# A cross-attention kernel: the last output-weight split one batch later, a norm quarter moved, another division of the beginning, another order of the tail

## The reference

```python
a = layer_norm(ctx) * gamma + beta          # B, T, D = 8, 512, 1024
Q = (x @ Wq.T), K = (a @ Wk.T), V = (a @ Wv.T)      # 16 heads of 64
scores = einsum('bhtd,bhsd->bhts', Q, K) * 64 ** -0.5
scores = where(mask, scores, -inf)
attn = softmax(scores)
out = einsum('bhts,bhsd->bhtd', attn, V)
return x + tanh(gate) * (out.reshape(B, T, D) @ Wo.T)
```

## Time and profile before

| | us |
|---|---|
| median of 3 runs (1995.44 to 1995.61) | 1995.55 |
| the profiled execution's own time | 2000.36 |
| its span (what the trace shows) | 1998.2 |
| PE busy | 1958.0 (98%) |
| DVE busy | 1613.8 (81%) |
| POOL busy | 1462.7 (73%) |
| ACT busy | 1344.3 (67%) |
| TensorE clock granted, mean | 0.994 |

### The profile page before, as it was taken

One profiled execution on the slowest core, in us unless ns is written; L12 is line 12 of the kernel. 1 busy time (PEld: TensorE's weight loads), 2 busy tenths in 40 slices (PEclk: granted clock), 3 DMA queues, 4 the chain that ended last, 5 costly groups with the idle time before them and its releaser, 6 DMA issues.

```text
span 1998.2 us, 26443 instructions
## 1 busy us (share of the span) xinstructions
PE 1958.0 (98%) x8720; PEld 1589.9 (80%) x8720; DVE 1613.8 (81%) x2082; ACT 1344.3 (67%) x2434; POOL 1462.7 (73%) x806
## 2 busy tenths in 40 slices
PE   6899999999999999999999999999999999999997
PEld 5787778888788887888888888888888888888886
DVE  7688768887788877888788887888878888778877
ACT  5768876578756686657865678665876568756554
POOL 4899996668865778666876669767697667966664
PEclk8999999999999999999999999999999999999999
DMA  7577544554355443554445543455433644435422
GB/s 264 174 252 242 189 172 167 220 180 140 130 194 188 168 170 112 212 197 142 151 149 194 191 168 119 163 197 182 175 129 130 253 151 150 154 124 191 164 93 106
DMA packets 136502, 341.96 MB, mean 171 GB/s; under 512 B 55856, under 2 KB 56880, under 8 KB 135472
## 3 DMA queue, kind: packets, MB, share of 16 engines
q1 hardware_dynamic: 136368, 340.28, 48.9%
HBM read 288.86 MB, written 51.36 MB: 170 GB/s over the span
## 4 chain that ended last, share of the span: by engine, by line
PE 79%; POOL 8%; ACT 6%; DVE 4%; issue 1%; DMA 1%; SPq 0%; ACTq 0%; DVEq 0%; POOLq 0%
PE pj L445 14%; PE pj L449 14%; PE pj L447 14%; PE sc L398 5%; PE sc L402 5%; PE sc L399 5%; PE sc L372 5%; PE sc L373 5%; PE pv L392 5%; PE pv L393 5%; POOL a_lo L1138 4%; DVE mq L821 2%; POOL p_lo L1104 2%; PE pj L381 1%; ACT prob L619 1%
## 5 line engine op out<-in xcount | busy, mean ns | idle before, releaser
L1104 POOL TENSOR_TENSOR p_lo<-prob,p_hi 128x1024 fp32r<-128x1024 f32 x255 | 611.4, 2408 | 188.1 <-ACT p_hi L624 188.1
L445 PE MATMUL pj<-a_hi,w_hi 128*128 128x512 f32 x1024 | 404.2, 395 | 7.7 <-DVE v_st L865 3.0
L449 PE MATMUL pj<-a_hi,w_lo 128*128 128x512 f32 x1024 | 401.3, 392 | 0.0
L447 PE MATMUL pj<-a_lo,w_hi 128*128 128x512 f32 x1024 | 401.0, 392 | 0.0
L821 DVE TRANSPOSE_TENSOR_REDUCE mq<-sc 128x32 f32<-128x1024 f32 x256 | 304.0, 1225 | 79.9 <-PE sc L373 79.1
L888 DVE SCALAR_TENSOR_TENSOR xy<-sc,tg_b,xy 128x1024 f32<-128x1024 f32 x244 | 306.2, 1273 | 31.6 <-PE sc L402 25.6
L619 ACT ACTIVATE prob<-prob 128x1024 f32<-128x1024 f32 x256 | 271.4, 1060 | 89.2 <-DVE prob L843 88.8
L843 DVE TENSOR_TENSOR prob<-sc,m_b 128x1024 f32<-128x1024 f32 x256 | 301.6, 1220 | 4.4
L1108 POOL TENSOR_TENSOR prob<-prob 128x1024 f32<-128x1024 f32 x126 | 302.1, 2398 | 0.0
L1115 POOL TENSOR_TENSOR r_b<-o,r_b 128x512 f32<-128x512 f32 x62 | 81.2, 1310 | 267.9 <-DVE r_b L860 267.9
L624 ACT CAST p_hi<-prob 128x1024 fp32r<-128x1024 f32 x256 | 269.5, 1053 | 3.5
(11 more groups left out here) (129 smaller groups left out, 3731.6 us busy)
## 6 DMA issues: line engine op xcount, KB each, us to landing
w_hi<-kept_hi SPq DMA_DIRECT2D x225, 512.0 KB, 3.7
w_lo<-kept_lo SPq DMA_DIRECT2D x225, 512.0 KB, 4.6
xy<-in_xT SPq DMA_DIRECT2D x32, 512.0 KB, 6.6
cx<-in_ctx SPq DMA_DIRECT2D x32, 512.0 KB, 7.4
kept_hi<-w_hi SPq DMA_DIRECT2D x32, 512.0 KB, 5.3
kept_lo<-w_lo SPq DMA_DIRECT2D x32, 512.0 KB, 6.0
out_y<-xy SPq DMA_DIRECT2D x7, 2048.0 KB, 9.8
w_raw<-in_wq SPq DMA_DIRECT2D x8, 512.0 KB, 5.1
```

Of the source, the lines that this page charges most:

```text
L445: pe.matmul(dst, w_hi[:, w, cols], s_hi[:, i], start=i == 0, stop=False)
L447: pe.matmul(dst, w_hi[:, w, cols], s_lo[:, i], start=False, stop=False)
L449: mm = pe.matmul(dst, w_lo[:, w, cols], s_hi[:, i], start=False, stop=i == KT - 1)
L1104: pool.tensor_tensor(p_lo[:, 2 * i:2 * i + 2], prob[:, h, 2 * i:2 * i + 2], f32(p_hi[:, 2 * i:2 * i + 2]), ALU.subtract).then_inc(pl_done, 1)
```

## The change

Five edits.

- The split of WO 7 leaves body 6. Its raw load goes out at the start of body 8, POOL makes its low part at the end of body 8, ACT its high part in body 9 ahead of the maxima, as for the other WO splits, into WO's own slot. SP's waits and stores around it move with it, and body 9 no longer loads WO 7 back.
- In batch 0 alone, the norm quarters of (5,0) and (6,0) stand behind `hand_out_maxima` on ACT instead of ahead of `gather_maxima`.
- In the beginning, DVE computes variance plus epsilon (two tiny instructions) and normalises with the mean itself, so that ACT has no `moments` there.
- In the beginning, the low parts of WK 0 and WV 0 are made by DVE (`first_split`), not by POOL; the two mask rows stand behind all of `a_low` and `q_low` instead of ahead of them, and `q_low` behind `a_low`; ACT casts slices 2, 4 and 6 instead of 2 and 5.
- In the tail, the last value matmuls and key sums stand ahead of the output pair that waits for DVE, and POOL makes the whole last low part of the probabilities (128 x 1024) where DVE had made half of it (L1035).

```diff
-FIRST_HIGH = (2, 5)
+FIRST_HIGH = (2, 4, 6)
...
-BODY_SPLITS += [[(WV, PAIRS - 1), (WO, PAIRS - 1), (WO, PAIRS - 3)], [(WO, PAIRS - 2)]]
+BODY_SPLITS += [[(WV, PAIRS - 1), (WO, PAIRS - 3)], [(WO, PAIRS - 2)], [(WO, PAIRS - 1)]]
...
         def out_split(k):
-
-            b, j = divmod(k - 1, PAIRS)
-            return b, WO, j - 1
+            return (0, WO, k - 2) if 2 <= k < PAIRS + 2 else (1, WO, 0)
...
             def batch(b):
                 for j in range(PAIRS):
                     k = b * PAIRS + j
+                    if k == PAIRS:
+                        m = NUMBER[WO, PAIRS - 1]
+                        sp.dma_start(w_raw[:, m % 2], wts[WO][PAIRS - 1]).then_inc(w_ld[m % 2], 16)
+                        keep_split(m - 1)
+                    if k == PAIRS + 1:
+                        keep_split(NUMBER[WO, PAIRS - 1])
                     load_kept(WV, (j + 1) % PAIRS, k)
                     exchange_sums(k - 1)
                     load_kept(WQ, (j + 2) % PAIRS, k)
                     load_kept(WK, (j + 2) % PAIRS, k)
-                    load_kept(WO, (j - 1) % PAIRS, k)
+                    if k == PAIRS + 1:
+                        sp.wait_ge(w_out[WO], 32 * PAIRS)
+                    if k > PAIRS:
+                        load_kept(WO, (j - 1) % PAIRS, k)
...
                 values(k, 1, 0)
                 pe.wait_ge(oadd_done, k * 2 + 1)
                 key_sums(1, 0, pv[0][:, 0])
+                values(k, 1, 1)
+                key_sums(1, 1, pv[0][:, 0])
                 pe.wait_ge(acc_done, 4 * k - 6)
                 out_pair(k - 2, 3, lower, done=False)
-                pe.wait_ge(plv_done, 1)
-                values(k, 1, 1)
-                key_sums(1, 1, pv[0][:, 0])
...
-                if (j, 0) in NORM and b < B - 1:
+                if (j, 0) in NORM and 0 < b < B - 1:
                     norm_quarter(b, NORM[j, 0])
                 if kind == "switch":
                     for i in range(KT // 2):
                         a_high(k, b, i)
                 gather_maxima(k, 0)
                 hand_out_maxima(k, 0)
+                if (j, 0) in NORM and b == 0:
+                    norm_quarter(b, NORM[j, 0])
...
                 split_w(b, WQ, j + 2)
                 if kind == "prepare":
-                    split_w(b, WO, PAIRS - 1, WQ)
                     for i in range(KT // 2, KT):
                         x_high(k, b, i, (b + 1) % 2)
...
-            moments(-1, 0)
-            moments(-1, 1)
             q_high(-1, 0)
             q_high(-1, 1)
...
-                dve.wait_ge(ph_done, k * 4 + 4)
-                dve.tensor_tensor(p_lo[:, 3], prob[:, 1, 3], f32(p_hi[:, 3]), ALU.subtract).then_inc(plv_done, 1)
                 gather(4 * k - 6, lower, 1)
...
+            def first_split(kind):
+                m = NUMBER[kind, 0]
+                dve.wait_ge(wlo_done, m)
+                dve.wait_ge(whi_done, m + 1)
+                dve.tensor_tensor(w_lo[:, kind], w_raw[:, m % 2], f32(w_hi[:, kind]), ALU.subtract).then_inc(wlo_done, 1)
...
+            first_split(WK)
+            for i in range(KT):
+                a_low(-1, i)
+                if i == KT // 2:
+                    first_split(WV)
+            q_low(-1, 0)
+            q_low(-1, 1)
             dve.wait_ge(mask_ld, 16)
...
-            q_low(-1, 0)
-            q_low(-1, 1)
-            for i in range(KT):
-                a_low(-1, i)
...
-            pool.wait_ge(z_done, TB)
-            for one in FIRST_SPLITS[1:]:
+            pool.wait_ge(wlo_done, 3)
+            for one in FIRST_SPLITS[3:]:
                 split_w(0, *one)
...
-                p_low(k, 0, 0)
-                p_low(k, 0, 1)
-                p_low(k, 1, 0)
-                pool.wait_ge(ph_done, k * 4 + 4)
-                pool.tensor_tensor(p_lo[:, 2], prob[:, 1, 2], f32(p_hi[:, 2]), ALU.subtract).then_inc(pl_done, 1)
+                for h in range(2):
+                    for i in range(2):
+                        p_low(k, h, i)
```

More of the change, by code:

```diff
@@ L168, in out_split, with w_arrived @@
         def out_split(k):
-            b, j = divmod(k - 1, PAIRS)
-            return b, WO, j - 1
-        def w_arrived(kind, pair):
-            return pair * 32 - 32 * (PAIRS - (3 if kind == WO else 1))
+            return (0, WO, k - 2) if 2 <= k < PAIRS + 2 else (1, WO, 0)
+        def w_arrived(pair):
+            return pair * 32 - 32 * (PAIRS - 1)
         block = es.enter_context(nc.Block())
@@ L188, in keep_w, with keep_split @@
                 kind, pair = ORDER[m]
-                slot, done = (WQ, w_out_last) if ORDER[m] == (WO, PAIRS - 1) else (kind, w_out[kind])
-                sp.dma_start(kept_hi[kind, pair], f32(w_hi[:, slot])).then_inc(done, 16)
-                sp.dma_start(kept_lo[kind, pair], f32(w_lo[:, slot])).then_inc(done, 16)
+                sp.dma_start(kept_hi[kind, pair], f32(w_hi[:, kind])).then_inc(w_out[kind], 16)
+                sp.dma_start(kept_lo[kind, pair], f32(w_lo[:, kind])).then_inc(w_out[kind], 16)
+            def keep_split(m):
+                sp.wait_ge(wlo_done, m + 1)
+                keep_w(m)
             def load_raw(kind, pair):
@@ L586, in _, with split_w @@
         def _(act):
-            def split_w(b, kind, pair, slot=None):
+            def split_w(b, kind, pair):
                 if not splits(b, kind, pair):
@@ L646, in moments @@
                 rows = slice(2 * pair, 2 * pair + 2)
-                act.wait_ge(bn_done, b * 3 * TB + (6 * TB if pair else 4 * TB + (2 if b < 0 else 3)))
+                act.wait_ge(bn_done, b * 3 * TB + (6 * TB if pair else 4 * TB + 3))
                 act.activation(vpe[:, rows], mv[:, rows, 1], ACT.Identity, bias=eps[:]).then_inc(stat_done, 1)
@@ L1069, in _ @@
                 row_moments(-1, pair)
+                rows = slice(2 * pair, 2 * pair + 2)
+                dve.wait_ge(bn_done, 6 * pair + 6)
+                dve.tensor_scalar(vpe[:, rows], mv[:, rows, 1], EPS, None, ALU.add).then_inc(stat_done, 2)
             for s in range(1, TB):
                 dve.wait_ge(rstd_done, s // 2 + 1)
-                dve.wait_ge(stat_done, s // 2 * 2 + 2)
-                dve.nop(nofuse=True)
-                dve.tensor_scalar(cx[:, s], cx[:, s], nmean[:, s:s + 1], rstd[:, s:s + 1], ALU.add,
+                dve.tensor_scalar(cx[:, s], cx[:, s], mv[:, s, 0:1], rstd[:, s:s + 1], ALU.subtract,
                                   ALU.mult).then_inc(z_done, 1)
+            first_split(WK)
[5 more added lines that the diff above has]
+            q_low(-1, 1)
             dve.wait_ge(mask_ld, 16)
@@ L1080, in _ @@
                                   ALU.add).then_inc(mrow_done, 1)
-            q_low(-1, 0)
-            q_low(-1, 1)
-            for i in range(KT):
-                a_low(-1, i)
+            k_low(-1, 0)
+            k_low(-1, 1)
             dve.wait_ge(tg_done, 1)
             mask_factor(-1, 0)
-            k_low(-1, 0)
-            k_low(-1, 1)
             run_bodies(body, last_body)
```

38 lines of the change are left out of this document (13 added, 25 removed).

## The result

| | before | after |
|---|---|---|
| median of 10 runs each, us | 1996.39 (1995.44 to 2001.98) | 2000.48 (1998.81 to 2002.65) |
| ratio, 95% interval | | 1.0020 (1.0012 to 1.0029) |
| profiled execution: own time, span, us | 2000.36, 1998.2 | 2001.88, 1999.9 |

The change makes the kernel 0.2% slower. That is 4.1 us, and it lies outside the forecast's range. Windows of the changed kernel, cut at the first scores matmul of each body as those of before were: the beginning, bodies 5, 6 and 7 of batch 0, the last body. The last row is a piece of body 6. Columns as in the earlier trace rows.

The account below looks back on a forecast made before the run. PE, busy 98% of the span, was taken as the bound, leaving only the beginning, batch 0 and last body. Beginning -3.4, middle (norm quarters and split) +0.9 and tail -0.8 gave -3.3: 1995.55 to 1992.3, range 1987.5 to 1997.0.

Parts of the forecast that it names:

- Taken off the median: Whole kernel: the summed -3.3, worked out on one profiled execution, was subtracted from the median 1995.55, giving 1992.3.
- the forecast's own 38.8: Beginning: scores of body 0 start at 38.8 instead of 42.29, 3.4 gained.
- The normalisation ends about when it did: Beginning: DVE takes over two tiny instructions from ACT without delaying the normalisation, so DVE's weight split ends near 21.0.
- The port rival: Beginning: POOL's WQ 1 split takes the port before DVE's last a_lo; no gain there, 1995.7 in all; chance 0.18.
- The norm quarters, "2.8 lost": Batch 0, bodies 5 and 6: the moved quarters delay ACT; 2.8 lost by mid body 6, bounds -2.0 and +4.6.
- The split, "-0.5 and -1.4": Bodies 6 and 7: moving the WO 7 split away gives back 0.5 and 1.4; bodies 8 and 9 lose nothing.
- The tail, "0.8 gained": Last body: PE's 1.27 wait for DVE's gather goes; 0.8 gained, bounds 0 to 1.3.
- The norm quarter is absorbed: Middle of batch 0: the moved quarter delays nothing, giving -3.6 instead of +0.9; 1987.8 in all; chance 0.28.
- where the prediction had 6: Beginning: PE's clock should rise about 6 us earlier, by 26, because PE works on from the transposes.
- The rival of 2001.0: Beginning: POOL first at the port and low clock for the whole v projection; with middle's upper bound, 2001.0; chance 0.06.

Follow-up runs that it names:

- experiment 7: Kernel before with the later WO 7 split and the new tail, keeping its old beginning and norm quarters; 1992.62 us, ratio 0.9982.
- experiment 11: Experiment 10 with POOL's low part of WQ 1 held until DVE's last a_lo has ended; 1991.93 us, ratio 0.9971.
- experiment 8: Changed kernel without the norm move, with POOL adding a negated mean made by ACT instead of subtracting; 1994.97 us, ratio 0.9994.
- experiment 10: Experiment 1 with the beginning's moments back on ACT and both POOL and DVE adding the negated mean; 1993.63 us, ratio 0.9984.
- experiment 12: Experiment 1 with POOL's low part of WQ 1 held until DVE's last a_lo has ended; 1994.62 us, ratio 0.9990.
- Experiment 4: Kernel before with only POOL's normalisation of context block 0 subtracting the mean instead of adding the negated mean; 2000.08 us, ratio 1.0017.
- experiment 1: Changed kernel with batch 0's norm quarters of (5,0) and (6,0) back ahead of the maxima; 1996.29 us, ratio 1.0001.
- experiment 5: Kernel before with only the new beginning, POOL's subtraction included; 1999.61 us, ratio 1.0015.
- experiment 13: Kernel before with only body 5's norm quarter of batch 0 moved behind the hand-out copies; 1997.21 us, ratio 1.0008.
- experiment 3: Kernel before with only the WO 7 split moved to bodies 8 and 9; 1994.93 us, ratio 0.9992.

## Why the prediction was wrong

From 1992.3 forecast to 2000.48 measured, in the order of the prediction's steps. By the runs: split and tail give -3.3 (experiment 7), the new beginning on top of them +3.7 (1996.29 - 1992.62), the norm move on top of that +4.2 (2000.48 - 1996.29). The sum is +4.6 against 1995.89, the median of before beside experiment 7; against 1996.39, beside which the change was timed, it is the +4.1. The sizes below are from different pairs of runs and do not add up to the tenth.

- **"Taken off the median": the step that failed first.** The sum put -3.3 of one profiled execution on a median that lay 4.8 below that execution's own time (2000.36 against 1995.55). The 42.29 from which the gain was counted was a property of that execution. In its the mask rows stood still beside POOL, 3.02 instead of 0.86, as the prediction describes it for a_lo. In the six experiments with the same beginning it ended at 39.0 to 39.7. Against that, the forecast's own 38.8 is a gain of 0.2 to 0.9, not 3.4, and the sum would have read 1995.55 - 0.5 + 0.9 - 0.8 = 1995.2. The 38.8 itself was sound: without subtraction, `vpe` and collision the scores came at 38.73 (experiment 11).
- **"The normalisation ends about when it did": wrong by 2.3.** 22.01 instead of 19.72. I had charged the change of the operand from `nmean` to `mv` at nothing, although it also changed add into subtract on POOL, and counted DVE's `vpe` as tiny. The first costs 2.6 on POOL, the second 0.6 on DVE and about 1.0 at the first transpose (experiments 8 and 10); together they cost 2.7 (experiments 11 and 12). All later steps of the beginning held: scores at 38.8 + 2.2 = 41.0. Experiment 4's 4.0 is more than the subtraction costs here, for it holds the mask rows' 2.92.
- **The port rival (0.18)** was right in mechanism and came in experiments 1, 5 and 10; PE's wait was 2.16 or 2.17 and its mean price 1.7 (experiments 11 and 12). In the profiled execution of the changed kernel DVE was first; how many of its other executions paid for it is not shown.
- **The norm quarters, "2.8 lost": right in two terms, wrong in one.** Body 5 lost 1.3, body 6's affines came 1.5 late, both as worked out. That ACT hands body 5's delay to body 6 was wrong, and changed no number: body 6's lateness is its own quarter's (experiment 13). The failed term is the clock. I took the low clock behind PE's 3 us wait, nine matmuls or so at 0.2, for the upper bound only. The wait was 2.86, and the clock fell with it in both traces that have the move in body 6, for 3.40 and 6.80 us. Beyond the 1.5 of lateness body 6 lost 1.2 in the first (39.66 - 37.00 - 1.5) and 2.6 in the second (40.71 - 36.62 - 1.5, against experiment 1). The 2.6 is all that the middle lost over its forecast, 3.5 against 0.9. The term belonged in the value, though the earlier trace rows were the wrong witness for it: the clock there was low not from the wait of 2.33 on but from 18.4 to 32.0, from within PE's wait of 3.85 ahead of its first transposes.
- **The split, "-0.5 and -1.4": right.** Body 6 gained 0.4 (37.00 to 36.61, experiment 3), body 7 1.46, and bodies 8 and 9 nothing to lose.
- **The tail, "0.8 gained": right.** The last body took 0.9 less.
- **"The norm quarter is absorbed"**, the rival that held most of the chance of a gain, fell: body 5 grew by 1.3 wherever its quarter was moved.

The low stretch of the clock in the beginning, before and with the change:

```profile
18.40:32.00 13.60, 9.26 (x32) 7.57 (x33) 12.45 (x15) 7.93 (x11) 4.79 (x2) 0.50 0.79 252
21.30:28.00 6.70, 5.84 (x24) 5.46 (x25) 5.50 (x9) 4.54 (x7) 0.00 (x0) 0.50 0.77 243
```

It came back 4.0 earlier than before, where the prediction had 6, at 28.0 instead of 26.

The rival of 2001.0 named the right total for other reasons, which is luck: it needed the clock low for the whole v projection. In the profiled execution v ran from a wait of only 0.45, and in experiment 1, where POOL was first, the clock was low for 3.4 us.

## What to carry to other kernels

Before a gain is read off one profile, put its own time beside the median; if it lies above, find the instruction that is longer than its like, for a gain counted from it exists only in that execution. Price every edit of an operation as a new instruction, even where shape and engine stay, and look at who waits for it. A PE wait of 2 to 3 us in a full stretch can cost its length and the clock behind it, so a forecast needs a term for both, and two engines whose two-input instructions start within 0.1 of each other are better ordered by a semaphore than left to chance.

## What the runs showed of the hardware

- POOL's tensor_scalar on 128x1024 f32 took 1.19 to 1.21 as add, multiply and 3.78 to 3.79 as subtract, multiply, in every run of either form. DVE did the subtracting form on two quarters in 1.54, against 1.53 for the adding one.
- POOL holds back more of DVE than the a_lo that the prediction thought of. The two mask rows (1x512) took 3.02 where POOL's weight split began at 20.55, ahead of the second of them at 20.6, and 0.86 where they were first. In experiment 7 the split began within them, at 20.56, and it was the split that took longer, 2.64 instead of 2.36; `vpe` (128x2) took 0.76 to 0.85 beside POOL's x_lo and 0.17 in its second instance. The Trainium skill (SBUF — State Buffer, "Who interferes with whom") counts tensor_scalar among the operations that can take the ports that DVE shares with GpSimd when their operands allow it, whoever issues first holding them. The mask rows and `vpe` agree, and so do the a_lo of 2.86 (POOL 0.05 ahead) and 0.69 (DVE ahead). I had read the rule for a_lo and not for the mask rows, which the earlier trace rows showed.
- With one and the same beginning the scores of body 0 started at 39.0 in one execution and at 42.3 in another.
- PE waits 2.04 to 2.08 for the low part of the values in body 0, in all 15 profiles. In 8 of them the clock then fell for 3.4 us and body 0 took 26.2; in the other 7 it did not, and body 0 took 24.6. Behind the waits of 2.16 or 2.17 in the beginning (3 profiles) and of 2.86 in body 6 (2 profiles) it fell each time.
